# The decay scan's operand as three bf16 parts, built by VectorE, in a Mamba-2, MLP and LoRA layer

## The chip, the cores and the metric

One Trainium2 chip; the kernel uses one of its cores. The metric is the device time of one execution in microseconds (us). TensorE (PE) multiplies, VectorE (DVE), ScalarE (ACT) and GpSimd (POOL) do elementwise work, and SyncE (SP) issues the DMAs. The weight loads of PE have a row name of their own, PEld.

## The reference, cut to what matters

The input is 2048 tokens of 512 values, as 8 sequences of 256. Each passes a layernorm, a Mamba-2 block, a gated MLP with 1792 inner channels, and a linear layer with a LoRA routed to one of 4 experts. The change concerns the decay of the Mamba-2 block, per chunk of 128 tokens and per head (4 heads):

```python
A = -jnp.exp(A_log)
a = (dt * A).reshape(B, c, Q, H).transpose(0, 1, 3, 2)      # Q = 128
cs = jnp.cumsum(a, axis=-1)
tri = jnp.tril(jnp.ones((Q, Q), bool))
Ldec = jnp.where(tri, jnp.exp(cs[..., :, None] - cs[..., None, :]), 0.0)
att = jnp.einsum('bchqn,bchkn->bchqk', Cc, Bc) * Ldec
Yd = jnp.einsum('bchqk,bchkp->bchqp', att, Xdt)
dec_end = jnp.exp(cs[..., -1:] - cs)
Yo = jnp.einsum('bchqn,bchpn,bchq->bchqp', Cc, prev, jnp.exp(cs))
```

## The kernel before

The kernel works on 8 groups, one sequence of 256 tokens each, as two tiles of 128 tokens. Its steps overlap three groups: step t does stage a (Mamba-2) of group t, stage b (the MLP) of group t-1 and stage c (linear, LoRA and the last norms) of group t-2. Group 0 has its stage a ahead of the first step, in `first()`, where the order of each engine is written out by hand. A step has 14 slots, one for each block f of 128 MLP channels. Each engine runs through the slots with its own instructions in a fixed order: in slot f first the MLP work of block f, then what the tables `A_AT`, `C_AT` and `NEXT_AT` put there. Engines meet by semaphores alone, and every engine runs its list strictly in order.

The MLP work of a slot: PE does the gate and up products of block f (`b_gu`, 24 products of 256 columns into gu) and the down products of block f-1 (`b_down`, 6 products of 512 columns into acc). ACT takes the gate's silu (`b_silu`, L670), DVE multiplies by the up half (`b_prod`, L1043), ACT rounds to f16 (`b_hi`, L680), and DVE makes the low half (`b_lo`, L1048), on which the down product of the next slot waits. A gate product of block f waits for `b_prod` of block f-2.

The decay: DVE makes dt and a (`a_dt`, last line L977) in slot 2, as 8 numbers per partition. POOL waits for them, and `a_scan_in` (L453) spreads them over the triangle: for each tile a 128x512 f32 tensor `ra`, which is the mask `tri` times a, for 4 heads. Then POOL does the same with dt (`a_tdt`, L461). PE's `a_dec` (slots 4 and 5) multiplies `ra` of tile 0 and tile 1 by the constant matrix `below` (zeros and ones), which gives the differences of the cumulative sums, and `ra` of tile 1 by `ones`. ACT takes the exponentials (`a_exp`, L638). DVE multiplies (`a_dec`, L987, and `a_att`, L996, slots 5 and 6), takes `w0` (L991), and POOL makes `xw` from `w0` (L476), which the state product of PE in slot 6 (`a_state`) needs. The memory of `ra` also holds the f16 rows `rows_1` that are transposed for the next group.

Also in these slots: DVE has `a_h0` (L919, two instructions) in slot 3 behind `b_lo`, then `c_stats2` (L885 to L887), and in slot 4 `c_h3` and `c_lo3` (L1073, L1095) behind `b_lo`. ACT has in slot 4, behind `b_hi`, `a_tok` (L627), a table load, two exponentials, `c_hi3` (L686), and a table load ahead of the silu of slot 5. In step 1, ACT and DVE also split the weights of the MLP (`prepare`, L560 and L870), three blocks of 128x512 a slot.

Of the kernel before, what the change touches and what calls it, by code (L numbers as in the profile page):

```python
# [20 lines left out]
F32 = mybir.dt.float32  # L21
# [7 lines left out]
P = 128  # L29
# [73 lines left out]
def build(nc, x, w_in, w_dt, w_out, w_gate, w_up, w_down, w_lin, w_gl, lora_b, cols, rows, ln_rows, out):  # L103
# [3 lines left out]
    with ctx:  # L107
        def sb(name, shape, dt=F32):
            return ctx.enter_context(nc.sbuf_tensor(name, shape, dt))
# [6 lines left out]
        def sem(name):  # L116
            if name not in made:
                made[name] = ctx.enter_context(nc.semaphore(name))
            return made[name]
# [37 lines left out]
        s_a = sb("small_a", [P, 2, TILES])  # L157
        dts = sb("dts", [P, 6, TILES, H])
        a_t = sb("a_t", [P, TILES, H])
        ra = sb("ra", [P, TILES, H, P])  # L160
        dec = sb("dec", [P, TILES, H, P])
        w0 = sb("w0", [P, H])

# [10 lines left out]
        first_conv = h1b[:].rearrange("p t d -> p (t d)").rearrange("p (c q) -> p c q", q=SEQ)  # L174

        rows_1, rows_2, rows_3 = [t.bitcast(F16).rearrange("p (t s d) -> p t s d", t=TILES, s=2)
                                  for t in (ra[:].rearrange("p t h q -> p (t h q)"),
                                            xbc[:, 0:4].rearrange("p c q -> p (c q)"),
                                            W[:, UNITS:UNITS + TILES].rearrange("p u n -> p (u n)"))]
        centered = dec[:].rearrange("p t h q -> p t (h q)")  # L180
# [138 lines left out]
        def prev(g, per, k, eng, s):  # L319

            if g > 0:
                eng.wait_ge(s, g * per - per + k)
# [94 lines left out]
        def _(pool):  # L417
# [30 lines left out]
            def a_scan_in(g):  # L448
                pool.wait_ge(sem("a_ready"), g + 1)
                for j in range(TILES):  # L450
                    if j == 0:
                        prev(g, 3, 3, pool, sem("dec_ps_ready"))
                    nc.gpsimd.tensor_tensor(ra[:, j], tri[:].unsqueeze(1).broadcast_to([P, H, P]),  # L453
                                            a_t[:, j].unsqueeze(2).broadcast_to([P, H, P]), ALU.mult)\
                        .then_inc(sem("ra_ready"), 1)
# [49 lines left out]
            def step(a, b, c):  # L505
                if c is not None:
                    chain_c.group(c)
                    norm_c(c, 1, 1.0)
                if b is not None:
                    b_copy(b)  # L510
                if a is not None:
                    a_xd(a)
                    a_scan_in(a)
                    a_tdt(a)
                if c is not None:
                    norm_c(c, 2, ACT_SCALE)
                if a is not None:
                    a_xw(a)
                    a_ce(a)
                    if a + 1 < GROUPS:  # L520
                        a_norm(a + 1)
                    a_rms(a)
                if c is not None:
                    norm_c(c, 3, 1.0)
                    chain_c.close()
# [241 lines left out]
        def _(dve):  # L767
            setup = Chain(dve, sem("dve_setup"), 0)
            setup.group(0)

            chain_a = Chain(dve, sem("dve_a"), 17)
            chain_stats = Chain(dve, sem("dve_stats"), 3)
            chain_c = Chain(dve, sem("dve_c"), 19)

# [187 lines left out]
            def a_dt(g):  # L962
# [4 lines left out]
                for c in (0.0, 1.0 / 3, -0.5, 1.0):  # L967
                    if c:
                        chain_a(nc.vector.scalar_tensor_tensor(t, t, c, e, ALU.add, ALU.mult))
                    else:  # L970
# [6 lines left out]
                nc.vector.tensor_tensor(a_t[:], dts[:, 4], neg_a[:].unsqueeze(1).broadcast_to([P, TILES, H]),  # L977
                                        ALU.mult).then_inc(sem("a_ready"), 1)

            def flat(t):  # L980
                return t.rearrange("p h q -> p (h q)")

# [163 lines left out]
            def c_out(g):  # L1146
                c_norm(g, 3, h3, h3, sem("n3_ready"))
                for j in range(TILES):
# [1 line left out]
                    nc.vector.tensor_tensor(h3[:, j], h3[:, j], x1[:, j], ALU.add).then_inc(sem("out_ready"), 1)  # L1150

            A_AT = {0: lambda g: a_conv(g, 0), 1: lambda g: (a_conv(g, 1), a_dtv(g)),
                    2: lambda g: (a_conv(g, 2), a_dt(g)), 3: lambda g: a_h0(g),
                    5: lambda g: (a_dec(g, 0), a_dec(g, 1), a_att(g, 0)), 6: lambda g: a_att(g, 1),
                    7: lambda g: (a_y(g, 0), a_y(g, 1)), 8: lambda g: a_h1(g, 0),
                    9: lambda g: a_h1(g, 1), 10: lambda g: a_weight(g), 11: lambda g: a_lo2(g)}
# [12 lines left out]
            def step(a, b, c):  # L1169
                if c is not None:  # L1170
                    chain_c.group(c)
                if a is not None:
                    chain_a.group(a)
                for f in range(FBLK):
                    if a == 1:
                        prepare(f)
                    if b is not None:
                        b_prod(b, f)
                        b_lo(b, f)
                    if a is not None and f in A_AT:  # L1180
                        A_AT[f](a)
                    if c is not None and f in C_AT:
                        C_AT[f](c)
                    if a is not None and a + 1 < GROUPS and f in NEXT_AT:
                        NEXT_AT[f](a + 1)
                if a is not None:
                    chain_a.close()
                if b is not None:
                    b_mlp(b)
                if c is not None:  # L1190
                    chain_c.close()
# [57 lines left out]
        def _(pe):  # L1249
# [95 lines left out]
            def a_dec(g, n):  # L1345

                if n < TILES:
                    if head(g):
                        pe.wait_ge(sem("conv_in_ready"), 1 + n)
                    else:  # L1350
                        pe.wait_ge(sem("sz_ready"), g * 2 + n + 1)
                    pe.wait_ge(sem("ra_ready"), g * 2 + n + 1)
                else:
                    pe.wait_ge(sem("exp_ready"), g * 3 + 1)
                mm(dec_bank(g, n)[:], (below if n < TILES else ones)[:], flat(ra[:, min(n, 1)]), True, True)\
                    .then_inc(sem("dec_ps_ready"), 1)

            def a_att(g, j):
                if j == 0:
# [257 lines left out]
```

## Time and profile before

| | us |
|---|---|
| median of 3 runs | 816.61 (816.28 to 816.96) |
| profiled execution | 815.18 |
| its span in the profile | 813.3 |
| PE busy, modelled | 762.6 (94%) |
| DVE busy | 485.3 (60%) |
| ACT busy | 331.6 (41%) |
| POOL busy | 154.1 (19%) |

A row of a timeline gives the start, the time to the end of the last of the merged instructions, the engine, the line, the operation, the tile written and those read, their shape and type, and in brackets how long the engine was idle before and who released it. An f32 matmul stands as two records on PE: so "x4" for two products. Matmul records overlap, so the pace of PE is read from the distance of starts.

### The profile page before, as it was taken

To read this page: it belongs to the slowest core of one execution; us is meant where nothing else is said; L and a number is where in the kernel's file an instruction comes from. 1 tells how busy PE (TensorE), PEld (TensorE's weight loads), DVE (VectorE), ACT (ScalarE), POOL (GpSimd) and SP (SyncE) were. 2 spreads that over 40 slices of the span, in tenths; PEclk is the share of its full clock that TensorE was granted. 3 is DMA by queue.
4 is the path that set the end of the run, shared out by engine and by line. 5 is a ranking of instruction groups with operands and counts; after the bars stand their busy time and mean duration, and the time that the engine had idled before them with its cause. 6 is when DMAs were issued, how large, how long until landed. Compare 5 with 4: busy or idle time off the path is not lost.

```text
span 813.3 us, 13857 instructions
## 1 busy us (share of the span) xinstructions
PE 762.6 (94%) x5558; PEld 536.6 (66%) x5558; DVE 485.3 (60%) x1109; ACT 331.6 (41%) x603; POOL 154.1 (19%) x197
## 2 busy tenths in 40 slices
PE   3994989989999999999999999999999999999945
PEld 3863866668666876577666876677656866577622
DVE  6877567877644765467645765467635664265163
ACT  2643476625523363325523363325523463222201
POOL 1421121205110331115110331015110330010010
PEclk9896899999999999999999999999999999999987
DMA  9941000110103120210103020310103010111010
GB/s 325 387 160 26 2 27 1 32 47 5 49 1 65 40 52 1 49 57 13 40 1 79 27 53 1 52 53 25 30 1 78 27 27 1 27 53 27 1 52 27
DMA packets 59936, 41.11 MB, mean 51 GB/s; under 512 B 45664, under 2 KB 45792, under 8 KB 59872
## 3 DMA queue, kind: packets, MB, share of 16 engines
q1 hardware_dynamic: 59872, 40.22, 17.6%
q8 instruction: 44, 0.72, 0.4%
q14 instruction: 20, 0.16, 0.1%
HBM read 25.01 MB, written 4.19 MB: 36 GB/s over the span
## 4 chain that ended last, share of the span: by engine, by line
PE 85%; DVE 7%; ACT 2%; DMA 2%; issue 1%; SPq 1%; POOL 0%; POOLq 0%; DVEq 0%; ACTq 0%
PE gu L1251 34%; PE wa L1251 25%; PE acc L1251 18%; PE wc L1251 7%; DVE weights L870 2%; DMA weights<-in_w_in 1%; DVE sg L1043 1%; DVE stats_c L885 0%; PE wa L1274 0%; DVE h L1073 0%; DMA xa<-in_x 0%; DMA ht<-ra 0%; ACT act L680 0%; PE wc L1466 0%; ACT weights L560 0%
## 5 line engine op out<-in xcount | busy, mean ns | idle before, releaser
L1251 PE MATMUL gu<-h2t,weights 128*128 128x256 f16 x2688 | 313.4, 273 | 0.6 <-DVE h2t L1037 0.6
L1251 PEld LDWEIGHTS gu<-h2t,weights 128*128 128x128 f16 x2688 | 260.9, 98 | 56.1 <-issue 19.7
L1251 PE MATMUL acc<-weights,act 128*128 128x512 f16 x672 | 163.4, 379 | 6.5 <-DVE act L1048 6.5
L1043 DVE SCALAR_TENSOR_TENSOR sg<-gu,bound,sg 128x256 f32<-128x256 f32 x112 | 53.6, 479 | 122.6 <-ACT sg L670 121.9
L670 ACT ACTIVATE sg<-gu,scale_inv 128x256 f32<-128x256 f32 x112 | 52.9, 472 | 160.3 <-PE gu L1251 160.1
L1251 PE MATMUL wa<-ht,weights 128*128 128x256 f16 x912 | 110.4, 280 | 3.7 <-DMA ht<-ra 3.7
L1251 PEld LDWEIGHTS acc<-weights,act 128*128 128x128 f16 x672 | 65.3, 98 | 63.6 <-DVE act L1048 8.3
L1251 PEld LDWEIGHTS wa<-ht,weights 128*128 128x128 f16 x912 | 91.6, 101 | 22.4 <-DMA ht<-ra 4.0
L680 ACT ACTIVATE act<-sg 128x256 f16<-128x256 f32 x112 | 46.6, 416 | 88.7 <-DVE sg L1043 88.7
L1048 DVE TENSOR_TENSOR act<-sg,act 128x256 f16<-128x256 f32 x112 | 50.5, 451 | 54.0 <-ACT act L680 54.0
L943 DVE SCALAR_TENSOR_TENSOR xbc<-wa,conv_ws,xbc 128x253 f32<-128x253 f32 (+1 forms) x132 | 57.3, 475 | 10.2 <-ACT xbc L597 8.6
L439 POOL TENSOR_SCALAR small_c<-mv_c 128x2 f32<-128x2 f32 x24 | 4.6, 192 | 290.3 <-DVE mv_c L887 290.3
L1251 PE MATMUL wa<-w_out_t,y 128*128 128x512 f32 x128 | 57.4, 592 | 0.0
L870 DVE SCALAR_TENSOR_TENSOR weights<-weights,scale_v 128x512 f16<-128x512 f32 x56 | 41.5, 796 | 6.7 <-ACT weights L560 6.6
L469 POOL TENSOR_SCALAR y<-xbc,rows_t 128x256 f32<-128x256 f32 x32 | 36.1, 1140 | 44.7 <-ACT xbc L608 44.7
L597 ACT ACTIVATE xbc<-wa,cols_t,conv_ws 128x256 f32<-128x256 f32 x48 | 24.4, 559 | 45.3 <-PE wa L1251 45.3
L1251 PEld LDWEIGHTS wa<-w_out_t,y 128*128 128x128 f32 x128 | 24.2, 190 | 25.5 <-issue 23.4
L1251 PE MATMUL wc<-weights,h3t 128*128 128x512 f16 x168 | 38.5, 379 | 0.0
L560 ACT ACTIVATE weights<-weights,scale_v 128x512 f16<-128x512 f32 x56 | 36.2, 710 | 0.8 <-DVE scale_v L820 0.5
L648 ACT ACTIVATE hn<-h 128x512 f32<-128x512 f32 x16 | 10.1, 631 | 61.5 <-DVE h L1011 61.5
L453 POOL TENSOR_TENSOR ra<-tri,a_t 128x512 f32<-128x512 f32 x16 | 19.2, 1218 | 69.4 <-DVE a_t L977 69.4
L1011 DVE TENSOR_TENSOR h<-wa,h 128x512 f32<-128x512 f32 x16 | 11.0, 690 | 35.3 <-PE wa L1251 35.3
(194 smaller groups left out, 800.4 us busy)
## 6 DMA issues: line engine op xcount, KB each, us to landing
xa<-in_x SPq DMA_DIRECT2D x8, 512.0 KB, 3.6
weights<-in_x SPq DMA_DIRECT2D x8, 512.0 KB, 3.7
out_x<-h SPq DMA_DIRECT2D x16, 256.0 KB, 2.2
weights<-in_w_in SPq DMA_DIRECT2D x5, 512.0 KB, 7.0
weights<-in_w_down SPq DMA_DIRECT2D x3, 768.0 KB, 14.1
weights<-in_w_gate SPq DMA_DIRECT2D x2, 1024.0 KB, 12.3
weights<-in_w_up SPq DMA_DIRECT2D x2, 1024.0 KB, 13.8
weights<-in_w_gate SPq DMA_DIRECT2D x2, 768.0 KB, 13.8
```

What stands on the lines that cost most here:

```text
L453: nc.gpsimd.tensor_tensor(ra[:, j], tri[:].unsqueeze(1).broadcast_to([P, H, P]), a_t[:, j].unsqueeze(2).broadcast_to([P, H, P]), ALU.mult)\
L469: nc.gpsimd.tensor_scalar(y[:, h], xbc[:, 0], rowt[:, 4 + h:5 + h], None, ALU.mult)\
L560: nc.scalar.activation(Wh[:, u, 0], W[:, u + SHIFT], ACT.Copy, scale=sv[:, t:t + 1])\
L597: nc.scalar.activation(xbc[:, c], src[:, m * SEQ:(m + 1) * SEQ], ACT.Identity, bias=conv_b[:, c:c + 1], scale=cw[:, c * TAPS + TAPS - 1:c ...
L670: nc.scalar.activation(sg[:, f % 2], GU[f % 2][:, 0:SEQ], ACT.Silu, scale=inv_gate)\
L680: nc.scalar.activation(act[:, slot(f), 0], sg[:, f % 2], ACT.Copy)\
L870: nc.vector.scalar_tensor_tensor(Wh[:, u, 1], W[:, u + SHIFT], sv[:, t:t + 1], Wh[:, u, 0], ALU.mult, ALU.subtract).then_inc(split, 1)
L943: ins = nc.vector.scalar_tensor_tensor(xbc[:, c, late:], conv_in(g, c)[:, 0:SEQ - late], cw[:, c * TAPS + k:c * TAPS + k + 1], xbc[:, c, l ...
L1011: nc.vector.tensor_tensor(h01[:, j], o_bank(g, j)[:], h01[:, j], ALU.add)\
L1043: nc.vector.scalar_tensor_tensor(sg[:, f % 2], GU[f % 2][:, SEQ:2 * SEQ], up_to_act, sg[:, f % 2], ALU.mult, ALU.mult).then_inc(sem("prod_ ...
L1048: nc.vector.tensor_tensor(act[:, slot(f), 1], sg[:, f % 2], act[:, slot(f), 0], ALU.subtract)\
L1251: return nc.tensor.matmul(dst, left, right, start=start, stop=stop)
```

## The change

In all groups but the first, VectorE makes the operand of the scan. In slot 2, behind `a_dt`, `a_parts_of` splits the 8 numbers a into three bf16 parts (round, subtract, round, subtract: four instructions, each waiting for the one before). In slot 3, between `b_lo` and `a_h0`, `a_scan_in` spreads the three parts of a tile over the triangle with one instruction of 128x1536, all bf16; the mask is read as the upper half of each f32 value of `tri`, a step of two bf16, and the parts with a step of zero along the triangle. POOL loses the two instructions of L453, and still waits for a before `a_tdt`. PE replaces each f32 product with three bf16 products of 512 columns into the same bank, with the upper halves of `below` or `ones` on the left. The new tensor takes three bf16 parts per value, and `ra` and `rows_1` lie in its memory. Group 0 stays as it was.

```diff
+        a_parts = sb("a_parts", [P, TILES, 3, H], BF16)
+        a_rest = sb("a_rest", [P, TILES, H])
+        scan = sb("scan_in", [P, TILES, 3, H, P], BF16)
...
                 if a is not None:
                     a_xd(a)
-                    a_scan_in(a)
+                    pool.wait_ge(sem("a_ready"), a + 1)
                     a_tdt(a)
...
+            def a_parts_of(g):
+
+                dve.wait_ge(sem("a_ready"), g + 1)
+                chain_p(nc.vector.tensor_copy(a_parts[:, :, 0], a_t[:]))
+                chain_p(nc.vector.tensor_tensor(a_rest[:], a_t[:], a_parts[:, :, 0], ALU.subtract))
+                chain_p(nc.vector.tensor_copy(a_parts[:, :, 1], a_rest[:]))
+                chain_p(nc.vector.tensor_tensor(a_parts[:, :, 2], a_rest[:], a_parts[:, :, 1], ALU.subtract))
+
+            def a_scan_in(g):
+                dve.wait_ge(sem("dec_ps_ready"), g * 3)
+                for j in range(TILES):
+                    nc.vector.tensor_tensor(
+                        scan[:, j].rearrange("p n h q -> p (n h) q"),
+                        upper(tri[:]).unsqueeze(1).broadcast_to([P, 3 * H, P]),
+                        a_parts[:, j].rearrange("p n h -> p (n h)").unsqueeze(2).broadcast_to([P, 3 * H, P]),
+                        ALU.mult).then_inc(sem("ra_ready"), 1)
...
-                    2: lambda g: (a_conv(g, 2), a_dt(g)), 3: lambda g: a_h0(g),
+                    2: lambda g: (a_conv(g, 2), a_dt(g), a_parts_of(g)),
+                    3: lambda g: (a_scan_in(g), a_h0(g)),
...
-                mm(dec_bank(g, n)[:], (below if n < TILES else ones)[:], flat(ra[:, min(n, 1)]), True, True)\
-                    .then_inc(sem("dec_ps_ready"), 1)
+                left, j = below if n < TILES else ones, min(n, 1)
+                if head(g):
+                    last = mm(dec_bank(g, n)[:], left[:], flat(ra[:, j]), True, True)
+                else:
+                    for part in range(3):
+                        last = mm(dec_bank(g, n)[:], upper(left[:]), flat(scan[:, j, part]), part == 0, part == 2)
+                last.then_inc(sem("dec_ps_ready"), 1)
```

On DVE, from the making of a in slot 2 to the statistics of slot 3, a step with all three stages. Before:

```order
L977 TENSOR_TENSOR a_t<-dts,neg_a 128x8
L1043 SCALAR_TENSOR_TENSOR sg<-gu,bound,sg 128x256
L1048 TENSOR_TENSOR act<-sg,act 128x256
L919 TENSOR_SCALAR h<-xa,mv_a,small_a 128x512 x2
L885 BN_STATS stats_c<-weights 128x6 x2
```

The same place of the changed kernel:

```order
L980 TENSOR_TENSOR a_t<-dts,neg_a 128x8
L986 CAST a_parts<-a_t 128x2x4
L987 TENSOR_TENSOR a_rest<-a_t,a_parts 128x8
L988 CAST a_parts<-a_rest 128x2x4
L989 TENSOR_TENSOR a_parts<-a_rest,a_parts 128x2x4
L1063 SCALAR_TENSOR_TENSOR sg<-gu,bound,sg 128x256
L1068 TENSOR_TENSOR act<-sg,act 128x256
L994 TENSOR_TENSOR scan_in<-tri,a_parts 128x1536 x2
L922 TENSOR_SCALAR h<-xa,mv_a,small_a 128x512 x2
L888 BN_STATS stats_c<-weights 128x6 x2
```

Four small instructions stand ahead of the MLP's work of slot 3, and two large ones behind it; all else on DVE keeps its order. On POOL, the same stretch (y is `a_xd`, the last row the second norm of stage c). Before:

```order
L469 TENSOR_SCALAR y<-xbc,rows_t 128x256 x4
L453 TENSOR_TENSOR ra<-tri,a_t 128x512 x2
L461 TENSOR_TENSOR hn<-tri,dts 128x512 x2
L439 TENSOR_SCALAR small_c<-mv_c 128x2
L440 TENSOR_TENSOR small_c<-small_c,minus_half 128x2
```

And of the changed kernel:

```order
L471 TENSOR_SCALAR y<-xbc,rows_t 128x256 x4
L463 TENSOR_TENSOR hn<-tri,dts 128x512 x2
L443 TENSOR_SCALAR small_c<-mv_c 128x2
L444 TENSOR_TENSOR small_c<-small_c,minus_half 128x2
```

The spreading of dt (hn, read later as tdt) now follows a directly. On PE, slots 4 and 5 of a step, before:

```order
L1339 MATMUL wa1<-ident,xbc 128x128 x3
L1251 MATMUL wa2<-ra,below 128x512
L1251 MATMUL wa0<-ra,below 128x512
L1251 MATMUL gu1<-h2t_1,weights 128x256 x24
L1251 MATMUL acc0<-weights,act 128x512 x3
L1251 MATMUL acc1<-weights,act 128x512 x3
L1251 MATMUL wa1<-xbc 128x512
L1251 MATMUL wa2<-ra,ones 128x512
```

And of the changed kernel:

```order
L1361 MATMUL wa1<-ident,xbc 128x128 x3
L1273 MATMUL wa2<-scan_in,below 128x512 x3
L1273 MATMUL wa0<-scan_in,below 128x512 x3
L1273 MATMUL gu1<-h2t_1,weights 128x256 x24
L1273 MATMUL acc0<-weights,act 128x512 x3
L1273 MATMUL acc1<-weights,act 128x512 x3
L1273 MATMUL wa1<-xbc 128x512
L1273 MATMUL wa2<-scan_in,ones 128x512 x3
```

The products stay where they were, three for one.

## Rows read from the trace of the kernel before

**Rows 1.** The page, busy time of each engine: us, share of span, instructions.

```profile
PE 762.6 (94%) x5558; PEld 536.6 (66%) x5558; DVE 485.3 (60%) x1109; ACT 331.6 (41%) x603; POOL 154.1 (19%) x197
```

**Rows 2.** Busy time by stages, a step with three stages: window, length, engines, PEclk, DMA.

```profile
310.00:400.00 90.00, 90.00 (x654) 63.17 (x652) 52.37 (x118) 37.02 (x68) 18.87 (x23) 1.00 0.16 36
```

**Rows 3.** Timeline of PE, 380 to 400.5 us, slots 4 to 6 of one step.

```profile
383.38 1.46 PE L1251 MATMUL acc<-weights,act 128*128 128x512 f16 x6
384.68 0.49 PE L1339 MATMUL wa<-ident,xbc 128*128 128x128 f32 x3
385.01 1.88 PE L1251 MATMUL wa<-ra,below 128*128 128x512 f32 x4
386.73 2.78 PE L1251 MATMUL gu<-h2t,weights 128*128 128x256 f16 x24
389.35 1.46 PE L1251 MATMUL acc<-weights,act 128*128 128x512 f16 x6
...
394.98 1.46 PE L1251 MATMUL acc<-weights,act 128*128 128x512 f16 x6
...
397.13 1.02 PE L1251 MATMUL wa<-hn,tok 128*128 128x512 f32 x2
```

**Rows 4.** Timeline of DVE, same step and window.

```profile
380.10 0.17 DVE L977 TENSOR_TENSOR a_t<-dts,neg_a 128x8 f32<-128x8 f32 x1
380.18 0.47 DVE L1043 SCALAR_TENSOR_TENSOR sg<-gu,bound,sg 128x256 f32<-128x256 f32 x1
381.14 0.53 DVE L1048 TENSOR_TENSOR act<-sg,act 128x256 f16<-128x256 f32 x1 [0.48 <-ACT act L680]
381.59 2.44 DVE L919 TENSOR_SCALAR h<-xa,mv_a,small_a 128x512 f32<-128x512 f32 x2
...
385.42 0.45 DVE L1043 SCALAR_TENSOR_TENSOR sg<-gu,bound,sg 128x256 f32<-128x256 f32 x1
386.36 0.42 DVE L1048 TENSOR_TENSOR act<-sg,act 128x256 f16<-128x256 f32 x1 [0.48 <-ACT act L680]
386.70 1.00 DVE L1073 TENSOR_SCALAR h<-weights,mv_c,small_c 128x512 f32<-128x512 f32 x2
...
392.93 0.43 DVE L1048 TENSOR_TENSOR act<-sg,act 128x256 f16<-128x256 f32 x1 [0.48 <-ACT act L680]
...
393.99 0.17 DVE L991 COPY w<-dec 128x4 f32<-128x4 f32 x1
...
399.37 0.52 DVE L1113 TENSOR_TENSOR eq<-logits,mx 128x8 f32<-128x8 f32 x1
```

**Rows 5.** Timeline of ACT, same step and window.

```profile
386.23 0.47 ACT L627 ACTIVATE tok<-wa 128x384 f32<-128x384 f32 x1
...
391.45 0.47 ACT L670 ACTIVATE sg<-gu,scale_inv 128x256 f32<-128x256 f32 x1
```

**Rows 6.** Timeline of POOL, same step and window.

```profile
380.35 2.22 POOL L453 TENSOR_TENSOR ra<-tri,a_t 128x512 f32<-128x512 f32 x2 [6.63 <-DVE a_t L977]
382.53 2.40 POOL L461 TENSOR_TENSOR hn<-tri,dts 128x512 f32<-128x512 f32 x2
...
394.24 1.54 POOL L476 TENSOR_TENSOR hn<-tok,w 128x512 f32<-128x512 f32 x1 [7.64 <-DVE w L991]
398.61 1.26 POOL L484 TENSOR_TENSOR hn<-hn,xbc 128x512 f32<-128x512 f32 x1 [2.83 <-ACT hn L638]
```

**Rows 7.** Groups of instructions by line and shape: busy us, mean ns, idle before.

```profile
L1083 DVE TENSOR_TENSOR weights<-weights,h 128x512 f32<-128x512 f32 x16 | 10.3, 682 | 0.0
```

**Rows 8.** Timelines of DVE and PE in step 1, 107.8 to 129 us.

```profile
108.00 3.63 DVE L870 SCALAR_TENSOR_TENSOR weights<-weights,scale_v 128x512 f16<-128x512 f32 x3
...
112.51 1.30 DVE L1048 TENSOR_TENSOR act<-sg,act 128x256 f16<-128x256 f32 x1 [0.48 <-ACT act L680]
...
114.64 2.06 DVE L870 SCALAR_TENSOR_TENSOR weights<-weights,scale_v 128x512 f16<-128x512 f32 x3
...
127.94 1.10 PE L1251 MATMUL wa<-hn,tok 128*128 128x512 f32 x2 [0.15 <-POOL hn L476]
```

More of the change, by code:

```diff
@@ L159, in build @@
         a_t = sb("a_t", [P, TILES, H])
-        ra = sb("ra", [P, TILES, H, P])
+        a_parts = sb("a_parts", [P, TILES, 3, H], BF16)
+        a_rest = sb("a_rest", [P, TILES, H])
+        scan = sb("scan_in", [P, TILES, 3, H, P], BF16)
+        ra = scan[:].rearrange("p t n h q -> p (t n h q)")[:, 0:2 * TILES * H * P].bitcast(F32)\
+            .rearrange("p (t h q) -> p t h q", t=TILES, h=H)
         dec = sb("dec", [P, TILES, H, P])
@@ L176, in build @@
         rows_1, rows_2, rows_3 = [t.bitcast(F16).rearrange("p (t s d) -> p t s d", t=TILES, s=2)
-                                  for t in (ra[:].rearrange("p t h q -> p (t h q)"),
+                                  for t in (ra.rearrange("p t h q -> p (t h q)"),
                                             xbc[:, 0:4].rearrange("p c q -> p (c q)"),
@@ L450, in a_scan_in @@
                 for j in range(TILES):
-                    if j == 0:
-                        prev(g, 3, 3, pool, sem("dec_ps_ready"))
                     nc.gpsimd.tensor_tensor(ra[:, j], tri[:].unsqueeze(1).broadcast_to([P, H, P]),
@@ L771, in _ @@
             chain_a = Chain(dve, sem("dve_a"), 17)
+            chain_p = Chain(dve, sem("dve_parts"), 4)
             chain_stats = Chain(dve, sem("dve_stats"), 3)
@@ L1173, in step @@
                     chain_a.group(a)
+                    chain_p.group(a - 1)
                 for f in range(FBLK):
```

## The prediction

> **What bounds the kernel now.** I read the page's busy times first. PE is busy 762.6 us of 813.3, DVE 485.3, ACT 331.6, POOL 154.1 [rows 1]. A share over the whole says little, so next the busy times of one steady stretch: from 310 to 400 us PE is busy 90.00 us of 90.00, at granted clock 1.00, while DVE has 52.37 and POOL 18.87 [rows 2]. PE never waits there. So two things count: how much PE work goes away, and whether PE begins to wait. The second is not a matter of DVE's 58%. It is a matter of how early DVE and ACT are at the few places where PE needs them, and for that I read the timelines of the four engines over slots 3 to 6 of one step [rows 3 to 6]. Steps 2 to 7 have this pattern. Step 1 has another neighbour, the splitting of weights [rows 8].
>
> **PE's products.** Two f32 products run from 385.01 to 386.73, 0.86 us each [rows 3]. Six 16-bit products of the same 512 columns run from 383.38 to 384.68, 0.217 us each [rows 3], so three bf16 ones take 0.65. The gain is 0.21 a product, three products in each of 7 groups: 21 x 0.21 = 4.4 us. It is real only where PE has no wait in its place. If all else were hidden, the profiled execution would go from 815.2 to 810.8.
>
> **POOL's part.** The two instructions of L453 go, and those for dt start at 380.35 in place of 382.53 [rows 6]. POOL is no bound, so this gains nothing of itself. But POOL and DVE hold each other up, and the rows show how. The comparison L1113 has 8 elements and takes 0.52 us; it starts at 399.37 under POOL's L484, which runs from 398.61 to 399.87, and ends 0.02 after it [rows 4, 6]. An instruction of the same size, the making of a, takes 0.17 with POOL idle [rows 4]. The two L919 take 2.44 us beside POOL, where two L1073 of the same shape, alone, take 1.00 [rows 4]. The step-1 weights split takes 3.63 beside POOL, 2.06 alone [rows 8]. So a DVE instruction of these forms waits until POOL's instruction ends, and POOL's next then waits for DVE's. One POOL instruction of 128x512 holds DVE for some 0.9 us (the two L453, 2.22 us, less 0.28 for the L1048 that came between and 0.14 of start). The products of gate and up, L1043, read PSUM and keep their 0.47 there [rows 4].
>
> The Trainium skill has this as a rule ("SBUF — State Buffer", section "SBUF: two separate sides"): a VectorE instruction in a two-port mode or with two SBUF inputs, and a GpSimd one, take turns at a shared port pair, each for its whole instruction. The rows agree with it.
>
> **The four small instructions on DVE.** Alone they would follow each other by 0.20 each and end 0.85 after a is ready at 380.27. But POOL starts at 380.35 with two instructions for dt. The first cast slips in ahead; the subtraction then waits for POOL until 381.39; POOL's second instruction takes over, and the second cast waits until about 382.3; the last subtraction ends at about 382.5. So L1043 of block 3 starts at 382.55, not at 380.18: 2.37 late. I take this value, since L1113 is the same kind and size. The lower end is 0.85, the upper end one more turn of POOL, 0.9 above. The L1048 that follows gets POOL idle and takes 0.42 in place of 0.53 [rows 4], leaving 2.26.
>
> **The two large instructions on DVE.** 8 elements take 0.17 us and 512 take 0.682 with two f32 inputs [rows 4, 7]: 1.02 to 1.03 ns an element, one element a cycle. 1536 elements make 0.17 + 1528 x 1.03 ns = 1.74; following each other they overlap by some 0.07, so 3.36 for both. No row has a two-input instruction with all operands of 16 bits. The bounds: one element a cycle, 3.36, or two, 1.76. I take the first, for here one input has a step of two and the other a step of zero, so that no neighbouring pair is read as one word.
>
> The Trainium skill ("Vector Engine (DVE) Microarchitecture Reference", section 5.1) says the same: the double rate wants a step of one on every operand, and one element read 16 times by a two-source instruction ran at the single rate. Its other page ("VectorE: DVE Perf Modes", the table of rates) lists bf16 tensor_tensor at twice the f32 rate, which by itself would speak for 1.76; no run here shows either yet.
>
> **What comes back.** The two L919 behind them find POOL idle: 1.00 in place of 2.44, a gain of 1.44 [rows 4].
>
> **DVE's delay at L1043 of block 4**, which stood at 385.42, is then 2.26 + 3.36 - 1.44 = 4.2 us.
>
> **Who waits for it.** The low half of block 4 ended at 386.78 and PE wanted it at 389.35: early by 2.57, and it now comes 4.2 late. ACT has its rounding of block 4 behind L1043, and behind that tok, a table load, the exponentials, `c_hi3` and a table load without a gap until the silu of block 5 at 391.45 [rows 5]. All of it moves by 4.2. The low half of block 5 ended at 393.36, PE wanted it at 394.98: early by 1.62 [rows 3, 4]. Then w0, POOL's xw, which ended at 395.78 [rows 6], and PE wanted it at 397.13 [rows 3]: early by 1.35, or 1.27 with the 0.08 of a handover (a ready at 380.27, POOL at 380.35). That is the last and smallest of the margins. PE can't make up for a wait here, because it has no slack. So it ends slot 6 later by 4.2 - 1.27 = 2.9 us, whatever it gained before: the 0.64 of its shorter products is inside that number and adds nothing. PE's waits in that step, walked through: 0.6 for block 3's low half, 1.1 for the scan operand of tiles 0 and 1, 0.4 for block 4, 1.2 for block 5, 0.3 for the state. That is 3.6, less 0.64. From slot 7 on DVE and ACT are caught up again: the next need, y, comes over 4 us of PE work later.
>
> **Step 1.** There the weights split alone takes 2.06 in place of 3.63 once POOL's instructions are over, and the L1048 of 1.30 takes 0.42 [rows 8]. The L919 had no POOL beside them, so nothing comes back. Delay: 2.3 - 1.6 - 0.9 + 3.4 = 3.2. PE already waits 0.15 for the state there [rows 8]: no margin, so 3.2 in full.
>
> **The sum.** 6 x 2.9 + 3.2 = 20.6. 815.2 + 20.6 = 835.8 for the profiled execution; it is 1.4 below the median of the runs, so **837 us**, 2.5% slower.
>
> **The rivals.**
> - *The small instructions aren't held up.* If POOL lets them through, the delay is 0.74 + 3.36 - 1.44 = 2.66 and a step costs 1.4; step 1 costs 1.8. Sum 10.2: 827. Against it stands L1113 in six of six steps; for it, that some of them have a single input.
> - *The large instructions run at two elements a cycle.* Delay 2.6, 1.3 a step, 1.6 in step 1, sum 9.6: 826. For it: all operands are of 16 bits. Against: the steps of two and zero.
> - *The cover holds (not slower).* Both of these together: delay about 1.06, under the margin of 1.27 at the state product, PE gets 0.2 a step: 815.6, and with the whole gain of 4.4, were the delay below 0.6, 812. It decides at a delay of 1.27 us at `a_state` in slot 6.
> - *More turns.* If POOL takes one more turn of 0.9 at each group, or the strided read costs more than a cycle: 837 + 7 x 0.9 = 843.
> - *The change doesn't do what it says:* three products aren't faster than one f32 product, for example through their weight loads. That costs at most what the gain was, and here the waits hide it: 837 still, as PE's place is set by DVE.
>
> **How the numbers follow.** My forecast 0.55 (with the last rival in it). No hold-up 0.16, double rate 0.12, cover holds 0.07, more turns 0.10. The range of the forecast alone is 832 to 841. From 822 to 844 the range takes in all but the case of the cover and the tails of the others: some 0.82. Changes under 0.2% (1.6 us) can't be told from none. Faster 0.05, same 0.03, slower 0.92.
>
> **What would show it.** L453 gone from POOL. The 128x1536 instructions at 1.74 us each (0.96 would be the double rate). The four small ones together 2.2 us from the end of a (0.85 if not held up), with POOL's two for dt above. L922 at 0.54 each. PE waiting before the down products of blocks 3, 4 and 5, before the first two scan products, and a little before the state, 3.6 us a step; a step 2.9 us longer, 93 to 94 us in place of 91. The granted clock stays at 1.00. The forecast is wrong if PE stays gapless in slots 4 to 6, or if the clock falls through the new waits, which would lengthen every product behind them.

## The result and the profile after

The changed kernel takes 838.9 us (median of 4 runs, 837.0 to 840.2), the kernel before 816.6 (816.3 to 817.0). The ratio is 1.0272, with a 95% interval from 1.0255 to 1.0288. The forecast was 837.0, from 822 to 844. The profiled execution of after is the longest of its four: 840.2 us, span 838.2. That of before, 815.2, lies 1.4 below the median.

The page, busy time of each engine (answers [rows 1]), and part 4, the chain that ended last:

```profile
PE 768.2 (92%) x5579; PEld 534.2 (64%) x5579; DVE 516.1 (62%) x1151; ACT 330.2 (39%) x603; POOL 135.4 (16%) x183
...
PE 67%; DVE 16%; ACT 9%; issue 4%; DMA 2%; POOL 2%; SPq 1%; POOLq 0%; DVEq 0%; ACTq 0%
```

DVE has 30.8 us more than in [rows 1], POOL 18.7 less. Only two thirds of the chain is PE's own work now (67%, against 85% on the page of before).

Busy time by stages, 93 us of it (answers [rows 2]):

```profile
318.00:411.00 93.00, 90.47 (x665) 63.25 (x663) 57.06 (x128) 36.52 (x67) 15.84 (x21) 1.00 0.15 35
```

The stretch is as long as one step. PE had no idle time in [rows 2]; here it is idle 2.5 us, at the same granted clock of 1.00. (The waits below add up to more, since a matmul record reaches past the distance of starts.) Timeline of PE in slots 3 to 6 of the step (answers [rows 3]):

```profile
392.21 2.78 PE L1273 MATMUL gu<-h2t,weights 128*128 128x256 f16 x24
395.54 1.47 PE L1273 MATMUL acc<-weights,act 128*128 128x512 f16 x6 [0.55 <-DVE act L1068]
396.85 0.49 PE L1361 MATMUL wa<-ident,xbc 128*128 128x128 f32 x3
397.30 0.81 PE L1273 MATMUL wa<-scan_in,below 128*128 128x512 bf16 x3
398.96 0.81 PE L1273 MATMUL wa<-scan_in,below 128*128 128x512 bf16 x3 [0.86 <-DVE scan_in L994]
399.61 2.78 PE L1273 MATMUL gu<-h2t,weights 128*128 128x256 f16 x24
402.55 1.47 PE L1273 MATMUL acc<-weights,act 128*128 128x512 f16 x6 [0.15 <-DVE act L1068]
...
409.11 1.47 PE L1273 MATMUL acc<-weights,act 128*128 128x512 f16 x6 [0.97 <-DVE act L1068]
...
411.63 1.10 PE L1273 MATMUL wa<-hn,tok 128*128 128x512 f32 x2 [0.19 <-POOL hn L478]
```

The waits stand where they were looked for: before the down products of blocks 3, 4 and 5, before the scan product of tile 1, and before the state. Three bf16 products take 0.65 us (398.96 to 399.61). The same stretch on DVE (answers [rows 4]):

```profile
391.54 0.17 DVE L980 TENSOR_TENSOR a_t<-dts,neg_a 128x8 f32<-128x8 f32 x1
391.74 0.17 DVE L986 CAST a_parts<-a_t 128x8 bf16<-128x8 f32 x1
391.95 0.91 DVE L987 TENSOR_TENSOR a_rest<-a_t,a_parts 128x8 f32<-128x8 f32 x1
392.89 0.97 DVE L988 CAST a_parts<-a_rest 128x8 bf16<-128x8 f32 x1
393.89 0.17 DVE L989 TENSOR_TENSOR a_parts<-a_rest,a_parts 128x8 bf16<-128x8 f32 x1
394.09 0.48 DVE L1063 SCALAR_TENSOR_TENSOR sg<-gu,bound,sg 128x256 f32<-128x256 f32 x1
...
395.40 3.42 DVE L994 TENSOR_TENSOR scan_in<-tri,a_parts 128x1536 bf16<-128x1536 bf16 x2
398.74 1.00 DVE L922 TENSOR_SCALAR h<-xa,mv_a,small_a 128x512 f32<-128x512 f32 x2
...
401.13 0.45 DVE L1063 SCALAR_TENSOR_TENSOR sg<-gu,bound,sg 128x256 f32<-128x256 f32 x1
```

And on POOL (answers [rows 6]):

```profile
391.79 2.04 POOL L463 TENSOR_TENSOR hn<-tri,dts 128x512 f32<-128x512 f32 x2 [6.63 <-DVE a_t L980]
...
409.94 1.54 POOL L478 TENSOR_TENSOR hn<-tok,w 128x512 f32<-128x512 f32 x1 [7.64 <-DVE w L1011]
```

The subtraction and the second cast, of 8 elements each, take 0.91 and 0.97 us, while their neighbours of the same size take 0.17. POOL's two instructions run from 391.79 to 393.83, and the second cast ends 0.03 behind them.

I measure both kernels from the start of the gate products of block 4. That is 392.21 after; in the timeline of PE of before it is the row ahead of [rows 3]:

```profile
380.76 2.78 PE L1251 MATMUL gu<-h2t,weights 128*128 128x256 f16 x24
```

| | before | after | later by |
|---|---|---|---|
| DVE starts L1043 (L1063) of block 4 | 4.66 | 8.92 | 4.26 |
| POOL's xw ends | 15.02 | 19.27 | 4.25 |
| PE starts the state product | 16.37 | 19.42 | 3.05 |

DVE's delay of 4.26 passes unchanged through ACT, DVE and POOL, and PE loses 4.26 less its margin of 1.2. The same distance of 19.41 or 19.42 stands in each of steps 2 to 7, and 16.36 or 16.37 before.

### The profile page after: what moved, and what is told of

It reads as the page before. It is cut to its first block, busy times and chain, and to the rows that moved or that the text cites. A ratio compares the mean times of both kernels' runs of the same rounds, so it can differ in the third digit from the quotient of the medians.

```text
span 838.2 us, 13927 instructions
## 1 busy us (share of the span) xinstructions
PE 768.2 (92%) x5579; PEld 534.2 (64%) x5579; DVE 516.1 (62%) x1151; ACT 330.2 (39%) x603; POOL 135.4 (16%) x183
## 4 chain that ended last, share of the span: by engine, by line
PE 67%; DVE 16%; ACT 9%; issue 4%; DMA 2%; POOL 2%; SPq 1%; POOLq 0%; DVEq 0%; ACTq 0%
PE gu L1273 25%; PE wa L1273 20%; PE acc L1273 14%; PE wc L1273 7%; DVE scan_in L994 3%; DVE sg L1063 1%; DVE weights L873 1%; DVE stats_c L888 1%; POOL hn L478 1%; ACT L672 1%; ACT L640 1%; ACT L623 1%; ACT act L682 1%; DMA weights<-in_w_in 1%; DVE h L922 1%
## 5 line engine op out<-in xcount | busy, mean ns | idle before, releaser
L1063 DVE SCALAR_TENSOR_TENSOR sg<-gu,bound,sg 128x256 f32<-128x256 f32 x112 | 53.6, 479 | 120.6 <-ACT sg L672 120.2
L1273 PEld LDWEIGHTS wc<-weights,h3t 128*128 128x128 f16 x168 | 16.4, 98 | 19.8
```

The costliest lines, as they stand in the source:

```text
L1063: nc.vector.scalar_tensor_tensor(sg[:, f % 2], GU[f % 2][:, SEQ:2 * SEQ], up_to_act, sg[:, f % 2], ALU.mult, ALU.mult).then_inc(sem("prod_ ...
L1273: return nc.tensor.matmul(dst, left, right, start=start, stop=stop)
```

## The experiments

Three of them ask where DVE's delay comes from, two where PE's gain went, two what margin there is, and the last four put the findings together. The kernel before ran beside each on the same chip; the ratio is to it, and "more" or "less" than before is worked out from the ratio. Beside the changed kernel its median was 816.6, beside the others 815.3 to 816.1, so a difference between two changed kernels is uncertain by up to 1.4 us. A step repeats far better inside a trace (91.20 or 91.21 us before, 94.33 or 94.34 after, from one state product to the next), so the distances in the traces are the sharper measure.

### tdt_late: POOL out of the way

```diff
-                    pool.wait_ge(sem("a_ready"), a + 1)
-                    a_tdt(a)
                 if c is not None:
                     norm_c(c, 2, ACT_SCALE)
+                if a is not None:
+                    pool.wait_ge(sem("ra_ready"), a * 2 + 2)
+                    a_tdt(a)
```

> The changed kernel, but POOL spreads dt only after the scan operand is built and, where stage c runs, after the second norm. So POOL is idle while DVE makes the parts and the scan operand. Theory (turns with POOL cost 1.4 to 1.5 us a step, and PE loses whatever DVE's delay at block 4 exceeds a margin of 1.2): the four small instructions take 0.85 in place of 2.2, DVE's delay falls from 4.26 to about 2.7, a step from plus 3.0 to plus 1.5, step 1 stays near plus 3 because POOL now runs beside L922 there; total 828. Rival (the small instructions' length is not what PE waits for, the large ones alone are): still 838 to 839.

Measured: 829.6 us, ratio 1.0174 (1.0154 to 1.0195). The changed kernel had 1.0272. Timelines of DVE and PE, the same place:

```profile
388.32 0.17 DVE L987 TENSOR_TENSOR a_rest<-a_t,a_parts 128x8 f32<-128x8 f32 x1
388.52 0.17 DVE L988 CAST a_parts<-a_rest 128x8 bf16<-128x8 f32 x1
```

```profile
388.58 2.78 PE L1273 MATMUL gu<-h2t,weights 128*128 128x256 f16 x24
...
406.46 1.10 PE L1273 MATMUL wa<-hn,tok 128*128 128x512 f32 x2 [0.19 <-POOL hn L478]
```

The same four instructions now take 0.17 each and follow each other by 0.20. By the medians 9.3 us are gone, by the ratios 8.0. No work was taken away; only the time changed at which POOL does its own. So most of what the small instructions cost in the changed kernel is the turns with POOL: 1.5 us in each of steps 2 to 7 (the state product starts 17.88 behind the gate products of block 4, against 19.42). Step 1 gains nothing (22.71 against 22.74), as expected. The rival of 838 falls.

### fast_rate and pairs: the length of the large instruction

`fast_rate` puts the 12 values of a triangle element side by side, and reads the mask as pairs of equal bf16 values. From group 1 on POOL too reads the mask as its bf16 half (not in the cut below; so in `pairs` and the kernels built on it):

```diff
-        scan = sb("scan_in", [P, TILES, 3, H, P], BF16)
+        scan = sb("scan_in", [P, TILES, P, 3, H], BF16)
...
+                nc.vector.tensor_copy(pairs(tri[:])[:, :, 0], upper(tri[:])).then_inc(sem("pairs_made"), 1)
...
-                        scan[:, j].rearrange("p n h q -> p (n h) q"),
-                        upper(tri[:]).unsqueeze(1).broadcast_to([P, 3 * H, P]),
-                        a_parts[:, j].rearrange("p n h -> p (n h)").unsqueeze(2).broadcast_to([P, 3 * H, P]),
+                        scan[:, j].rearrange("p q n h -> p q (n h)").rearrange("p q (m two) -> p q m two", two=2),
+                        pairs(tri[:]).unsqueeze(2).broadcast_to([P, P, 6, 2]),
+                        a_parts[:, j].rearrange("p n h -> p (n h)").rearrange("p (m two) -> p m two", two=2)
+                        .unsqueeze(1).broadcast_to([P, P, 6, 2]),
...
-                        last = mm(dec_bank(g, n)[:], upper(left[:]), flat(scan[:, j, part]), part == 0, part == 2)
+                        last = mm(dec_bank(g, n)[:], upper(left[:]), scan[:, j, :, part].rearrange("p q h -> p h q"), part == 0, part == 2)
```

> The changed kernel with the same values in another layout: the triangle outside, the 12 parts inside, and the mask stored twice per value, so that every operand of the large DVE instruction has 16 bits and an innermost step of one. Theory (the large instruction runs one element a cycle because of its steps of two and zero): here about 0.97 us in place of 1.75, DVE's delay 2.7 in place of 4.26, a step plus 1.5 in place of plus 3.0, total 827. PE then reads its right operand at a step of 24 bytes, at 0.217 us a product as before. Rival 1 (one element a cycle whatever the steps): 1.75 us and 839. Rival 2 (PE reads the wide step more slowly): products above 0.217, total above 830 though DVE is faster.

Measured: 867.1 us, ratio 1.0629 (1.0600 to 1.0658), some 28 us longer than the changed kernel. The groups of instructions by line and shape, and the timeline of PE:

```profile
L1003 DVE TENSOR_TENSOR scan_in<-tri,a_parts 128x1536 bf16<-128x1536 bf16 x14 | 12.7, 952 | 0.0
```

```profile
409.28 5.52 PE L1284 MATMUL wa<-scan_in,below 128*128 128x512 bf16 x6
414.62 4.24 PE L1284 MATMUL gu<-h2t,weights 128*128 128x256 f16 x24
418.69 1.46 PE L1284 MATMUL acc<-weights,act 128*128 128x512 f16 x6
```

DVE's part came out as forecast: 0.95 us in place of 1.75. The second rival came out too, and it is larger. Six products take 5.34 us, 0.89 each in place of 0.217. Behind them the 24 gate products take 4.07 in place of 2.62, and the windows show why:

```profile
409.00:414.60 5.60, 5.60 (x10) 0.95 (x9) 4.38 (x11) 2.46 (x4) 0.92 (x2) 0.96 0.30 94
414.60:418.60 4.00, 4.00 (x25) 2.94 (x24) 1.29 (x2) 3.13 (x5) 0.00 (x0) 0.62 0.17 35
```

The granted clock of PE is 0.62 in this stretch, between its two levels of 1.2 and 2.4 GHz, though PE had no gap ahead of it: what it did before were the slow products. It is so in all seven steps: the 24 gate products behind the slow ones take 3.6 to 4.9 us. This run didn't say whether the step of 24 bytes or the layout as such was at fault, so `pairs` lays the values out as (part and pair of heads, triangle, 2). PE then reads at a step of 4 bytes:

```diff
+        scan = sb("scan_in", [P, TILES, 6, P, 2], BF16)
...
+                        scan[:, j], pairs(tri[:]).unsqueeze(1).broadcast_to([P, 6, P, 2]),
+                        a_parts[:, j].rearrange("p n h -> p (n h)").rearrange("p (m two) -> p m two", two=2)
+                        .unsqueeze(2).broadcast_to([P, 6, P, 2]),
...
+                        last = mm(dec_bank(g, n)[:], upper(left[:]),
+                                  scan[:, j, 2 * part:2 * part + 2].rearrange("p m q two -> p m two q"), part == 0, part == 2)
```

> The changed kernel with the values laid out in pairs of heads: (part and pair of heads, triangle, 2), so that DVE's operands all have an innermost step of one, and PE reads its right operand at a step of 4 bytes, not 24. Theory (PE slowed only through the 24-byte step of fast_rate, DVE's delay counts beyond a margin of 1.2): DVE's large instruction 0.95, PE's three products 0.68, as where POOL's f32 values were read at that step; delay 2.7, a step plus 1.5, total 827. Rival (the double-rate instruction or the layout has some other cost, or the length of the large instruction doesn't count): 838 or more.

Measured: 826.6 us, ratio 1.0139 (1.0119 to 1.0159). Both operands hold their rate:

```profile
L1003 DVE TENSOR_TENSOR scan_in<-tri,a_parts 128x1536 bf16<-128x1536 bf16 x14 | 12.7, 953 | 0.0
...
L1283 PE MATMUL wa<-scan_in,below 128*128 128x512 bf16 x42 | 10.6, 387 | 0.0
```

(387 ns is the record of one product; `fast_rate` has 1069 there, the changed kernel 377 to 379.) So the step of the read was what cost PE its pace, and 1.6 us less of DVE time in a step are worth 11 to 12 us over seven groups.

### pe_only and f32_products: where PE's gain went

`pe_only` is the kernel before with three bf16 products for one. All three read the upper halves of the values, so it leaves the lower parts out of the result and keeps only the shape of the work:

```diff
-                mm(dec_bank(g, n)[:], (below if n < TILES else ones)[:], flat(ra[:, min(n, 1)]), True, True)\
-                    .then_inc(sem("dec_ps_ready"), 1)
+                left, right = below if n < TILES else ones, flat(ra[:, min(n, 1)])
+                if head(g):
+                    last = mm(dec_bank(g, n)[:], left[:], right, True, True)
+                else:
+                    for part in range(3):
+                        last = mm(dec_bank(g, n)[:], upper(left[:]), upper(right), part == 0, part == 2)
+                last.then_inc(sem("dec_ps_ready"), 1)
```

> The kernel before, with POOL building the f32 operand as it did, and only PE changed: three bf16 products on the upper halves of the values, in place of one f32 product (the lower parts of the values are left out of the result). Theory (a product costs 0.65 in place of 0.86 and PE has no wait to hide it): 21 x 0.21 = 4.4 us less, 812.2. Rival (three weight loads or the steps of two eat the gain): 816 to 817.

Measured: 811.6 us, ratio 0.9959 (0.9943 to 0.9975), which is 3.3 us less. PE's timeline:

```profile
383.13 1.52 PE L1251 MATMUL wa<-ra,below 128*128 128x512 bf16 x6
384.49 2.78 PE L1251 MATMUL gu<-h2t,weights 128*128 128x256 f16 x24
```

Six products take 1.36 here, 0.227 each: reading every second bf16 value costs 0.01 a product over the 0.217 of [rows 3]. Three make 0.68, so the gain is 0.18 a product and 3.8 in all, within the interval of what was measured. The gain is real where PE doesn't wait.

`f32_products` is the changed kernel with one f32 product as before. It reads the first part's bytes as f32, so it leaves the decay out and keeps the shape of the work:

```diff
-                if head(g):
-                    last = mm(dec_bank(g, n)[:], left[:], flat(ra[:, j]), True, True)
+                if True:
+                    v = flat(ra[:, j]) if head(g) else scan[:, j, 0].rearrange("p h q -> p (h q)").bitcast(F32).unsqueeze(1).broadcast_to([P, 2, 2 * P])
+                    last = mm(dec_bank(g, n)[:], left[:], v, True, True)
                 else:
                     for part in range(3):
```

> The changed kernel with DVE's work as it is, but one f32 product in place of three bf16 ones (it reads the first part's bytes as f32, so the decay is not computed). Theory (PE's place after slot 6 is set by DVE's delay, the gain of the shorter products is swallowed by the waits): 839, as changed. Rival (gain and waits add up): 4.4 more, 843.

Measured: 838.4 us, ratio 1.0282 (1.0261 to 1.0302), against 1.0272 of the changed kernel: the same. The state product stands 19.42 behind the gate products of block 4 in both. In the changed kernel PE's saving is worth nothing. Its timeline shows the longer products taking the place of the waits:

```profile
397.33 1.10 PE L1273 MATMUL wa<-scan_in,below 128*128 128x512 f32 x2 [0.57 <-DVE scan_in L994]
...
400.90 1.47 PE L1273 MATMUL acc<-weights,act 128*128 128x512 f16 x6
...
407.47 1.47 PE L1273 MATMUL acc<-weights,act 128*128 128x512 f16 x6 [0.76 <-DVE act L1068]
```

The waits are 0.57, under 0.1 and 0.76 where the changed kernel has 0.86, 0.15 and 0.97.

### dose_4 and dose_2: the margin by itself

Both are the kernel before with idle statistics on DVE in slot 3 (four or two, `range(4)` or `range(2)`):

```diff
+            def a_dose(g):
+                for k in range(4):
+                    nc.vector.bn_stats(spare[:, k], lnt[:, 0])
...
-                    2: lambda g: (a_conv(g, 2), a_dt(g)), 3: lambda g: a_h0(g),
+                    2: lambda g: (a_conv(g, 2), a_dt(g)), 3: lambda g: (a_h0(g), a_dose(g)),
```

> The kernel before, with four more DVE instructions in slot 3 behind a_h0, statistics of a constant row that nothing reads, some 0.6 us each, which do not hold up POOL: a dose of 2.4 us of DVE time. Theory (margin of 1.2 at the state product, none in step 1): 6 x 1.2 + 2.4 = 9.6, total 826. Rival 1 (DVE has 42% idle time and hides it): 816.6. Rival 2 (every us of delay counts in full): 7 x 2.4 = 16.8, total 833.

> The kernel before with two more DVE instructions of 0.6 us in slot 3, a dose of 1.2 us. Theory (margin of 1.2 in steps 2 to 7, none in step 1): 6 x 0 + 1.2, so 817 to 817.5 where before is 816. Rival (no margin, proportional): half of the 9.3 of dose_4, 820.7.

Measured: `dose_4` 825.3 us, ratio 1.0121 (1.0102 to 1.0139), 9.9 us more. `dose_2` 817.9 us, ratio 1.0023 (1.0009 to 1.0036), 1.9 us more. Twice the dose costs about five times as much, so there is a threshold, and it lies near 1.2 us. The timelines of DVE and PE of `dose_4`, and that of PE of `dose_2`:

```profile
387.99 2.46 DVE L925 BATCH_NORM_STATS2 spare<-ln_rows_t 128x6 f32<-128x512 f32 x4
```

```profile
384.80 2.78 PE L1256 MATMUL gu<-h2t,weights 128*128 128x256 f16 x24
...
399.81 1.47 PE L1256 MATMUL acc<-weights,act 128*128 128x512 f16 x6 [0.63 <-DVE act L1053]
...
402.33 1.10 PE L1256 MATMUL wa<-hn,tok 128*128 128x512 f32 x2 [0.19 <-POOL hn L477]
```

```profile
380.48 2.78 PE L1256 MATMUL gu<-h2t,weights 128*128 128x256 f16 x24
...
396.85 1.07 PE L1256 MATMUL wa<-hn,tok 128*128 128x512 f32 x2
```

In `dose_4` the state product starts 17.53 behind the gate products of block 4, against 16.37 before: 1.16 later for a dose of 2.38 (the statistics of stage c start at 390.37, the first dose at 387.99). The margin is 1.22, and no changed scan operand or bf16 product is in this kernel. In `dose_2` it starts 16.37 behind, as without a dose, in every one of steps 2 to 7, and only in step 1 it comes later, by the whole dose (20.55 against 19.36).

### Putting it together: two misses of order, then a gain

`pairs_tdt_late` is `pairs` with POOL's edit of `tdt_late`. `pairs_both_late` also moves `a_h0` out of slot 3:

```diff
-                    3: lambda g: (a_scan_in(g), a_h0(g)),
+                    3: lambda g: a_scan_in(g),
...
-                    6: lambda g: a_att(g, 1),
+                    6: lambda g: (a_att(g, 1), a_h0(g)),
```

> Pairs, and POOL's spreading of dt behind the second norm. Theory: DVE's delay at block 4 is 0.74 + 1.76 - 1.44 = 1.06 us, under the margin of 1.2, so PE keeps 0.1 to 0.2 a step; step 1 has no margin and costs about 1.6. Total 815 to 817, the same as before. Rival (no margin, each us of DVE's delay costs PE one): 1.06 x 7 = 7.4 less the products' gain, 820.

> As pairs_tdt_late, and a_h0 (two instructions of DVE) moved from slot 3 to slot 6, behind the attention's last product. Theory: DVE's delay at block 4 is 0.74 + 1.76 - 2.44 = 0.1 us, under every margin, so the whole gain of the shorter products stays: 21 x 0.18 = 3.8, total 812 to 813, faster than both kernels. Rival (a_h0 is then late for the load of the next group's input or for the sum in slot 8): 817 or more.

Measured: `pairs_tdt_late` 817.9 us, ratio 1.0023 (1.0013 to 1.0034), 1.9 over before and 0.9 over the upper end of what was expected. In steps 2 to 7 the state product is 0.07 earlier than before (16.30 behind the gate products, against 16.37), but it takes as much longer behind its wait, and a step is 91.21 in both kernels. In step 1 it is 1.8 later (21.12 against 19.36): POOL's moved work stands beside `a_h0` and the split of the weights there, which take 1.72 and 2.85 in place of 0.99 and 2.06. `pairs_both_late` took 856.3 us, ratio 1.0504 (1.0484 to 1.0524), where 812 was expected. The waits, and the timelines of SP and PE, name the cause:

```profile
PE wc L1283 <- DMA h3t<-weights: 34.7, 5, 7.0
```

```profile
416.00 0.39 SPq L370 DMA_DIRECT2D xa<-in_x  x1
416.49 3.19 SPq L365 DMA_TRANSPOSE h3t<-weights  x2
```

```profile
421.78 0.90 PE L1283 MATMUL wc<-gl_w,h3t 128*128 128x36 f16 x24 [6.84 <-DMA h3t<-weights]
```

SP's list is in order as well. The load of the next input waits for `a_h0`, and the transposes of stage c stand behind that load. I moved the step on DVE and overlooked the queue that waits for it. Behind each of the five waits the 24 gate products also take 3.7 to 3.8 us (here from 422.52 to 426.29) in place of 2.62, and the granted clock from 421.7 to 424.0 is 0.50. A step is 99.0, against 90.67 in `best`. `best` mends that. SP's two issues change places, `a_h0` goes to the end of slot 5, and POOL waits for block 4's low half:

```diff
-                if following:
-                    a_x(a + 1)
                 if c is not None and not alone(c):
                     c_t3(c)
+                if following:
+                    a_x(a + 1)
...
-                    5: lambda g: (a_dec(g, 0), a_dec(g, 1), a_att(g, 0)), 6: lambda g: a_att(g, 1),
+                    5: lambda g: (a_dec(g, 0), a_dec(g, 1), a_att(g, 0), a_h0(g)), 6: lambda g: a_att(g, 1),
...
+                    pool.wait_ge(sem("act_ready"), (a - 1) * FBLK + 5)
+                    a_tdt(a)
```

`best_plain` is the same order with the layout of the changed kernel.

> As pairs_both_late, but SP issues the transposes of stage c before the load of the next input (which waits for a_h0), a_h0 stands at the end of slot 5, and POOL spreads dt behind block 4's low half in every step. Theory (pairs_both_late lost 7 us a step only because the transposes stood behind that load in SP's queue; DVE's delay at block 4 is now 0.1 in steps 2 to 7 and under zero in step 1): PE has no new wait and keeps 3.8 us; 811 to 812.5 where before is 816. Rival (another chain, such as the load of the next input for slot 8, is late by then): PE waits in slots 8 to 13, 816 or more.

> The same order with the layout of the changed kernel, so DVE's large instruction takes 1.75 us, not 0.95, and PE's products 0.65 for three. Theory: DVE's delay at block 4 is 0.74 + 3.36 - 2.44 = 1.7 us, 0.5 over the margin, and about 1.8 in step 1 without margin: 816 + 6 x 0.5 + 1.8 = 821. Rival (the order alone, with POOL out of the way, would have been enough): 811 to 812.

Measured: `best` 812.6 us, ratio 0.9961 (0.9948 to 0.9975), 0.4% faster than the kernel before. The wait for the transposes is gone from its trace; the three moves were made together, so none is priced alone. `best_plain` 821.9 us, ratio 1.0075 (1.0061 to 1.0090), as forecast. The order alone isn't enough, the double rate alone (`pairs`, 826.6) isn't either. Timeline of PE in `best`:

```profile
380.80 2.78 PE L1283 MATMUL gu<-h2t,weights 128*128 128x256 f16 x24
...
396.62 1.02 PE L1283 MATMUL wa<-hn,tok 128*128 128x512 f32 x2
```

The state product starts 15.82 behind the gate products of block 4, 0.55 earlier than before (16.37). That is three times 0.18.

## Why the prediction was right

- **What bounds the kernel.** Right. PE is the bound, and the margins of the engines that feed it decide. The doses show it without the change: 2.38 us of DVE time cost 1.16 a step, half of it nothing in steps 2 to 7.
- **The products.** 0.65 for three against 0.86 was right (398.96 to 399.61), and so was that it adds nothing here (`f32_products`). Its worth elsewhere is 3.3 to 3.8 us.
- **The four small instructions.** 2.37 later was forecast for L1043 of block 3. It starts 2.55 behind the start of a, where it started 0.08 behind it: 2.47. The turns fell on the second and the third of them, as walked through, and `tdt_late` takes the cost away by moving POOL alone. The rule of the Trainium skill that stands in the prediction ("SBUF — State Buffer", "SBUF: two separate sides"), turns at a shared port pair by whole instructions, agrees with the trace: 0.91 and 0.97 for 8 elements.
- **The large instructions.** 1.74 each was forecast, 1.75 measured; 3.36 for both, and L922 starts 3.34 behind the first (395.40 to 398.74). The reason given, the steps of two and zero, is borne out by `pairs`: the same 1536 elements with innermost steps of one take 0.95. The runs changed both steps together, so which of the two would do it alone is not shown. The Trainium skill ("Vector Engine (DVE) Microarchitecture Reference", section 5.1) asks for a step of one on every 16-bit operand, and both times agree with it.
- **L922.** 1.00 for two, as forecast.
- **DVE's delay** of 4.2 came out as 4.26, the loss of 2.9 a step as 3.05. The margin was put at 1.27; it is 1.22 by `dose_4`, and 1.35 less a handover of 0.15 from POOL to PE (xw ends at 411.48, PE starts at 411.63) makes 1.20; the prediction had taken 0.08 for the handover, from another pair of engines.
- **The waits.** Forecast 0.6, 1.1, 0.4, 1.2, 0.3. By the distances of starts, less the work between, they are 0.7 (395.54 less 392.21 and 2.62), 1.1 (0.1 ahead of the first scan product, 1.0 ahead of the second), 0.3, 1.1 and 0.4.
- **The sum.** 20.6 was forecast, 22.3 lies between the medians. The state product, 3.05 late, also takes 0.93 in place of 0.86 behind its wait (411.63 to 412.56), so a step is 3.13 longer: 94.34 against 91.21. Six steps make 18.8, 1.4 more than forecast. In step 1 the state product starts 22.74 behind the gate products of block 4, 19.36 in the kernel before (108.58 to 127.94, answers [rows 8]): 3.4, forecast 3.2. Together 22.2. The two traces lie 24.9 us apart, because the profiled execution of after is the longest of its four and that of before a short one. After is 1.8 behind already when a is made in step 1 (109.72 against 107.91), before any changed instruction runs. The gate products of block 4 of step 1 start anywhere from 107.0 to 110.4 in the thirteen traces, and at 108.74 in `f32_products`, which is the same as the changed kernel up to there. Another 1.0 arises behind step 7, where the last 54 us of after have a lower granted clock than the last 53 of before:

```profile
760.00:813.30 53.30, 32.45 (x197) 18.02 (x195) 22.65 (x57) 8.10 (x16) 3.52 (x8) 0.84 0.09 30
```

```profile
784.00:838.20 54.20, 33.36 (x197) 18.29 (x194) 22.66 (x57) 8.10 (x16) 3.52 (x8) 0.79 0.09 30
```

  So the 1.8 is not the change's, and the 1.0 is not shown to be.
- **The clock.** "The granted clock stays at 1.00" was right in steps 2 to 7 and wrong in step 1. Timeline of PE and a window of the changed kernel there:

```profile
110.39 2.78 PE L1273 MATMUL gu<-h2t,weights 128*128 128x256 f16 x24
115.71 2.74 PE L1273 MATMUL acc<-weights,act 128*128 128x512 f16 x6 [2.54 <-DVE act L1068]
...
123.25 1.47 PE L1273 MATMUL acc<-weights,act 128*128 128x512 f16 x6 [0.39 <-DVE act L1068]
...
133.13 1.10 PE L1273 MATMUL wa<-hn,tok 128*128 128x512 f32 x2 [0.19 <-POOL hn L478]
```

```profile
115.70:117.00 1.30, 1.29 (x4) 0.47 (x5) 1.30 (x1) 1.30 (x4) 0.00 (x0) 0.50 0.00 0
```

  Six down products take 2.54 (to 118.25) where they take 1.30 elsewhere, at a granted clock of 0.50, the level of 1.2 GHz, behind a wait of 2.54. It cost next to nothing: PE waits for DVE again at 123.25, and would only have waited longer. The kernel before has a wait of 2.51 at that place and no lower clock. Of the traces with a wait of 2.50 to 2.54 there, `f32_products` and `fast_rate` show the slow products too, and `pairs`, `pe_only` and both doses don't. Why it falls in some and not in others stays open.

The rivals: *not held up* and *double rate* each need something that the traces contradict, but the prices given for them, 827 and 826, are near what `tdt_late` (829.6, with step 1 no cheaper) and `pairs` (826.6) measured when their condition was made true. *The cover holds* had its deciding point at a delay of 1.27. `pairs_tdt_late` was built to lie at 1.06 in steps 2 to 7 and came out 1.9 over before, because step 1 lost 1.8; the 0.2 a step that the rival gives PE did not come either (a step of 91.21 in both). *More turns*: POOL took its two turns and no third, since L989 runs in 0.17.

## What to carry to other kernels

Work moved to an engine that is 60% busy is not free, and not paid in full either. Go through the places where the bound engine needs that engine's results, and take the one where the result was least early (here the state product, by 1.2 us; it was 2.6 and 1.6 at the down products before it). What the delay exceeds that by is lost once per loop, whatever the bound engine saved ahead of that place. When a step is moved, follow everyone who waits for it, DMA queues included; `a_h0` moved by three slots cost some 40 us through SP's order. And before a small instruction is put beside GpSimd's work, look for an instruction of its size in the trace that already stands there.

## What the runs showed of the hardware

- TensorE's moving operand of bf16: 512 columns take 0.217 us at a step of 2 bytes, 0.227 at 4 bytes, 0.89 at 24 bytes. The Trainium skill ("SBUF — State Buffer", section "Door 1: The DMA port swizzle") speaks of lines of 16 bytes that want at least two accesses each. A step of 24 bytes gives each line at most one, a step of 4 gives four, and the runs agree with that.
- The granted clock fell to 0.62 behind such slow products, with PE never idle, so a slow operand costs twice: 5.34 us for six products, and 1.45 more for the 24 behind them (`fast_rate`, 409.28 to 418.69).
- A two-input DVE instruction of 16-bit operands runs at nearly twice the rate already when two adjacent elements are innermost and a step of zero stands further out: 1536 elements in 0.95 us, against 1.75 where one operand has a step of two and the other of zero.
- A one-input cast of 8 elements waits for GpSimd just as a two-input one does: 0.97 us in place of 0.17. The first cast, which starts before POOL does (391.74 against 391.79), keeps its 0.17.
